# A five-stage image and text model on one core: which expert outputs are combined on TensorE, and how linear attention's contraction is split

## The reference

```python
# mixture of experts: G=8 groups of S=192 tokens, capacity C=60 a group and expert
gate, idx = top_k(softmax(x @ w_router), 2)
dispatch = one_hot(place_of_token_in_expert, C)
combine = dispatch * gate
expert_out = relu(einsum('gsec,gsd->egcd', dispatch, x) @ wi) @ wo
h = h + einsum('gsec,egcd->gsd', combine, expert_out)
# linear attention, 12 heads of 16
q, k, v = layernorm(h) @ w_qkv.T
q, k = q / max(sum_over_tokens|q|, eps), k / max(sum_over_tokens|k|, eps)
h = h + (q @ (k.T @ v)) @ w_proj.T + b_proj
```

## Time and profile before

| | us |
|---|---|
| median of three runs | 353.85 |
| lowest and highest of them | 352.6 and 359.36 |
| profiled execution, its own time | 351.75 |
| its span (first to last instruction) | 349.9 |

### The profile page before, as it was taken

The page is one execution under the profiler, slowest core; times in us unless marked ns, Lnnn a source line. Parts: engine busy times, 40 slices in busy tenths (PEclk is TensorE's granted clock), DMA queues, the critical chain, the costliest instruction groups (busy, mean ns, idle before and its releaser), DMA issues.

```text
span 349.9 us, 9294 instructions
## 1 busy us (share of the span) xinstructions
PE 319.5 (91%) x3966; PEld 216.6 (62%) x3966; DVE 193.6 (55%) x636; ACT 112.5 (32%) x218; POOL 52.4 (15%) x100
## 2 busy tenths in 40 slices
PE   3999899887788889999999999999998999998595
PEld 3876468655665336574747484756676576777465
DVE  2817487999999992141431110202045887789864
ACT  1233635665741352222222213030202232333250
POOL 8403233100111000000020000000028811101100
PEclk9999999999999999999999999999999999999899
DMA  7985011333120000505050505000002200000005
GB/s 254 350 238 146 5 37 36 116 108 125 54 55 3 2 0 2 153 7 156 3 157 2 157 2 157 4 21 24 0 25 65 53 20 0 3 2 0 2 0 135
DMA packets 16485, 23.45 MB, mean 67 GB/s; under 512 B 3995, under 2 KB 12573, under 8 KB 16445
## 3 DMA queue, kind: packets, MB, share of 16 engines
q1 hardware_dynamic: 14972, 21.10, 20.1%
q0 software_dynamic: 576, 1.18, 1.3%
q10 hardware_dynamic: 896, 0.59, 0.7%
HBM read 20.11 MB, written 2.75 MB: 65 GB/s over the span
## 4 chain that ended last, share of the span: by engine, by line
PE 64%; DVE 16%; SPq 8%; issue 4%; DMA 3%; POOL 2%; ACT 2%; DVEq 0%; POOLq 0%
PE banks L755 18%; PE banks L770 18%; PE banks L810 3%; PE banks L264 3%; SPq L288 2%; PE banks L818 2%; SPq L340 2%; PE banks L654 2%; PE banks L857 2%; PE banks L847 2%; PE banks L522 2%; DVE sb_onehot_combT L1729 2%; DVE sb_stat L1551 2%; POOL sb_onehot_combT L478 2%; SPq L286 1%
## 5 line engine op out<-in xcount | busy, mean ns | idle before, releaser
L755 PE MATMUL banks<-sb_tok_xeT,sb_wi_sl 128*128 128x480 f32 (+1 forms) x192 | 64.9, 590 | 1.1 <-ACT sb_tok_xeT L1264 1.1
L770 PE MATMUL banks<-sb_wo_sl,sb_attn_hidT_attn 128*60 128x192 f32 x768 | 64.1, 327 | 0.0
L770 PEld LDWEIGHTS banks<-sb_wo_sl,sb_attn_hidT_attn 128*60 128x60 f32 x768 | 52.9, 133 | 12.5 <-issue 4.0
L1279 ACT ACTIVATE sb_attn_hidT_attn<-banks 128x480 f32<-128x480 f32 x48 | 25.6, 569 | 95.7 <-PE banks L755 95.7
L755 PEld LDWEIGHTS banks<-sb_tok_xeT,sb_wi_sl 128*128 128x128 f32 (+1 forms) x192 | 24.8, 187 | 37.7 <-issue 35.8
L1777 DVE COPY sb_w_tok_e_out<-banks 60x384 f32<-60x384 f32 x16 | 8.9, 555 | 61.9 <-PE banks L770 61.6
L522 PE MATMUL banks<-sb_tok_xeT 128*32 128x193 f32 (+1 forms) x512 | 23.4, 328 | 0.0
L1779 DVE COPY sb_onehot_combT<-banks 60x384 f32<-60x384 f32 x16 | 8.9, 555 | 22.1 <-PE banks L770 22.0
L522 PEld LDWEIGHTS banks<-sb_tok_xeT 128*32 128x32 f32 (+1 forms) x512 | 15.8, 109 | 5.9 <-issue 2.3
L810 PE MATMUL banks<-sb_w_kv,sb_xnT 96*128 96x384 f32 x48 | 17.6, 497 | 1.0 <-ACT sb_xnT L1290 1.0
L1183 ACT ACTIVATE sb_onehot_combT<-sb_tok_xeT 128x1024 f32<-128x1024 f32 x8 | 8.5, 1059 | 21.7 <-DMA sb_tok_xeT<-in_xhalo 21.7
(11 more groups left out here) (262 smaller groups left out, 516.9 us busy)
## 6 DMA issues: line engine op xcount, KB each, us to landing
sb_wo_sl<-in_wo SPq DMA_DIRECT2D x8, 576.0 KB, 4.7
sb_tok_xeT<-in_xin SPq DMA_DIRECT2D x8, 448.0 KB, 5.4
sb_wi_sl<-in_wi SPq DMA_DIRECT2D x8, 288.0 KB, 3.1
sb_wi_sl<-in_wi SPq DMA_DIRECT2D x24, 96.0 KB, 3.1
sb_w_tok_e_out<-in_wtok SPq DMA_DIRECT2D x2, 960.0 KB, 7.2
expert_rows<-sb_onehot_combT SPq DMA_DIRECT2D x8, 192.0 KB, 4.4
sb_w_tok_e_out<-in_wtok SPq DMA_DIRECT2D x1, 576.0 KB, 8.4
out<-sb_h SPq DMA_DIRECT2D x8, 72.0 KB, 2.0
```

The source lines that it names most:

```text
L755: mm = nc.tensor.matmul(PS[:, banks[z], 0:SLOTS], lhs, rhs.rearrange("k g c -> k (g c)"), start=first, stop=not first)
L770: mm = nc.tensor.matmul(PS[64 * z:64 * z + CAP, 4 + hf, pr * D:(pr + 1) * D], hidT[:, e % 2, f, g * CAP:(g + 1) * CAP], wo_sl[:, q, f], st ...
L1279: nc.scalar.activation(hidT[:, e % 2, f], PS[:, HID_BANKS[(e * (FT // 2) + f // 2) % 2][f % 2], 0:SLOTS], ACT.Relu).then_inc(sem("hidT"), 1)
```

## The change

- `JC` is 1: only group 0 is combined on TensorE. Groups 1, 2 and 3 (`ROW_GROUPS = 3`) go through memory: rows of three groups are stored for each expert (288 KB in place of 192 KB), and 18 fetches are made, in the order of the groups. Three blocks of combine weights are built and turned in place of six, and `combine(1, ...)` with its two additions is gone. `keep_expert` makes four copies of 192 columns for the first half of an expert's results (group 0 to `e_out`, group 1 to `rows_out`) in place of two of 384. `rows_out` lies in another buffer and is cleared later.
- Linear attention's features are split as 128 + 64. `turn_linear` makes three transposes a block (the last 64 features are laid down twice, in partitions 0 to 63 and 64 to 127), the weights are loaded in the same way (15 transfers in place of 9), and `linear_keys_values` and `linear_queries` first do all products over 128 features and then those over 64, with neighbours in different halves of the array. Keys and values of a group are now one step of three blocks.
- `soft_norm` has two small operations ahead of the normalizing in place of five; the power is now of D times the variance, to +1/2 (the small constants change from TINY to TINY_VAR with it).
- PSUM banks, the waits ahead of TensorE's steps and the lists of TensorE, ScalarE, VectorE and GpSimd are new from the last expert on.

```diff
-JC = 2
+JC = 1
+ROW_GROUPS = J - JC
-LIN_T_BANKS, LIN_Q_BANKS, LIN_KV_BANKS = (0, 1), (1, 3), (1, 0, 4)
-PROD_BANK, SUM_BANK, LIN_O_BANKS, PROJ_BANKS = 4, 0, (1, 2), (3, 2)
+LIN_T_BANKS, LIN_Q_BANKS, LIN_KV_BANKS = (0, 1), (2, 3), (0, 4, 7)
+PROD_BANK, SUM_BANK, LIN_O_BANKS, PROJ_BANKS = 4, 1, (1, 2), (5, 3)
...
             def turn_linear(j):
+                src = xn_b[j % 2]
                 for blk in range(NB):
                     pe.wait_ge(sem("b_xn"), NB * j + blk + 1)
-                    for kh in range(2):
-                        mm = flip(PS[0:HD, LIN_T_BANKS[kh], blk * 128:(blk + 1) * 128], xn_b[j % 2][:, blk, kh * HD:(kh + 1) * HD])
+                    cols = slice(blk * 128, (blk + 1) * 128)
+                    flip(PS[:, LIN_T_BANKS[0], cols], src[:, blk, 0:128])
+                    flip(PS[:, LIN_T_BANKS[1], cols], src[:, blk, D - 128:D])
+                    mm = flip(PS[0:DT, LIN_T_BANKS[1], cols], src[:, blk, 128:D])
                 mm.then_inc(sem("b_xnT_ps"), 1)
-            def linear_keys_values(j, blk):
+            def linear_keys_values(j):
                 pe.wait_ge(sem("b_xnT"), j + 1)
-                for kh in range(2):
-                    mm = nc.tensor.matmul(PS[:, LIN_KV_BANKS[blk], 0:2 * D], xnT[:, kh, blk * 128:(blk + 1) * 128],
-                                          w_kv1[:, kh], start=(kh == 0), stop=(kh == 1))
-                mm.then_inc(sem("b_kv_ps"), 1)
+                for blk in range(NB):
+                    nc.tensor.matmul(PS[:, LIN_KV_BANKS[blk], 0:2 * D], xnT[:, 0, blk * 128:(blk + 1) * 128], w_kv1[:, 0],
+                                     start=True, stop=False)
+                for blk in range(NB):
+                    rows = slice(blk % 2 * DT, (blk % 2 + 1) * DT)
+                    nc.tensor.matmul(PS[:, LIN_KV_BANKS[blk], 0:2 * D], xnT[rows, 1, blk * 128:(blk + 1) * 128], w_kv1[rows, 1],
+                                     start=False, stop=True).then_inc(sem("b_kv_ps"), 1)
...
             for e in range(E):
                 expert_inner(e)
-                if 0 < e < 4:
-                    turn_comb(2 * e - 2)
-                    turn_comb(2 * e - 1)
+                if 0 < e < 3:
+                    for i in ((0, 1), (2,))[e - 1]:
+                        turn_comb(i)
                 expert_outer(e)
...
                         if hf == 0:
-                            ve.tensor_copy(e_out[64 * (e % 2):64 * (e % 2) + CAP, z:z + 3:2, e // 2], src).then_inc(sem("e_out"), 1)
+                            ve.tensor_copy(e_out[64 * (e % 2):64 * (e % 2) + CAP, z, e // 2], src[:, 0])
+                            ve.tensor_copy(mine[:, 0], src[:, 1]).then_inc(sem("e_out"), 1)
                         else:
-                            ins = ve.tensor_copy(rows_out[64 * z:64 * z + CAP, e % 2], src)
+                            ins = ve.tensor_copy(mine[:, 1:3], src)
...
-                then(ve.tensor_tensor(st[:, 6], mv[:, :, 1], st[:, 3], ALU.mult))
-                then(ve.scalar_tensor_tensor(st[:, 7], st[:, 6], float(D) ** 0.5, st[:, 2], ALU.mult, ALU.mult))
-                then(ve.tensor_scalar(st[:, 8], st[:, 7], L2_EPS, None, ALU.add))
-                then(ve.reciprocal(st[:, 9], st[:, 8]))
-                then(ve.tensor_tensor(st[:, 4], st[:, 9], st[:, 2], ALU.mult))
+                then(ve.scalar_tensor_tensor(st[:, 6], st[:, 2], L2_EPS, st[:, 3], ALU.mult, ALU.add))
+                then(ve.reciprocal(st[:, 4], st[:, 6]))
```

247 lines of the change are left out of this document (125 added, 122 removed).

## The result

| | before | changed |
|---|---|---|
| median of 7 runs each, us | 353.85 | 355.99 |
| lowest and highest, us | 352.05 to 359.36 | 354.36 to 357.76 |
| ratio of the two, 95% interval | | 1.0074 [1.0044, 1.0104] |
| profiled execution: own time, span, us | 351.75, 349.9 | 355.87, 354.0 |
| mean granted clock of that execution | 0.995 | 0.976 |

The change costs 0.7%, some 2.6 us, where 351.0 us was forecast; the time lies above the range of 346.5 to 355.5. In this table and the next the medians, lowest and highest times are of all runs, while the ratios leave out the slow ones, those over 1.5% above the fastest of the same kernel (one of the kernel before here, two of e4's four, nine of the 30 of the kernel before behind h1 to h4).

A forecast was written before the change was run, and what follows sets the result against it. GpSimd's queue of fetches and scales, not TensorE, was taken to decide what a removed combine is worth. Terms behind the experts summed to 0, experts saved 1.5: 351.75 - 1.5 = 350.2, plus 0.85 gave 351.0 us, range 346.5 to 355.5.

The forecast's parts named there:

- TensorE's clock: Wait ahead of first linear-attention turn: a clock fall worth 1.4 to 2 us, all but 0.3 hidden, left out of sum.
- Rival 3: Linear attention, groups 0 and 1: half clock set off by the 7.3 us wait stays; 356.5 us, chance 0.1.
- signs of being wrong: Idle under 4 us before first turn; half-clock stretch over 5 us; VectorE late at last norm by over 1 us.
- signs of being right: About 7 us idle before first turn; scale two fetches later; K/V(2) released by GpSimd's scale; K/V 3.4 to 3.5 us.
- The late fall may go: Near the last norms: idle time shrinks to about 2 us, which would give back 1.3 us; left out of sum.
- Store and first fetch, norm scale of group 0: Behind the experts: store +0.3 us, scale behind four fetches, TensorE waits 7.3 us, the step 3.0 us late.
- Contraction: Linear attention's 128+64 split: overlapping half products save net 0.56 us a group, 2.2 in all; K/V 3.45 for 3.95.
- Rival 2: Linear attention: halves don't overlap, a group costs 0.39 us more instead of 0.56 less; 353.4 us, chance 0.07.
- Groups 1 to 3: Linear attention: fetch queue and scales make group 1 1.9 us late; queries(3) done at 313.3 us against 311.3.
- Soft experts: Soft mixture after queries(3): shorter norm chain wins back 2.0 us; last norm ends at 328.8 where it was 328.88.
- rival 1: Whole kernel: TensorE is the bound throughout, its saved 8.3 us shows in full; 343.5 to 345 us, chance 0.15.
- Rival 4: Row fetches: 12 more blocks land later than 3.8 us behind their start, delaying groups 1 and 2; 352 us, chance 0.08.

The follow-up runs named there:

- e4: Changed kernel with groups 0 and 1 combined on TensorE and two groups' rows fetched, as before; 355.33 us, ratio 0.9918.
- h1: Kernel before, waits filled, with the first linear-attention turn moved ahead of group 1's combining, so TensorE waits; 356.18 us, ratio 1.0067.
- h4: Changed kernel as it is, measured again on another chip; 357.55 us, ratio 1.0088 to the kernel before.
- e1: Changed kernel with seven unread products filling the wait between combine(0) and the first linear-attention turn; 355.08 us, ratio 1.0012.
- f1: Changed kernel with unread products filling TensorE's waits at three places, seven of them behind combine(0); 350.88 us, ratio 0.9943.
- e3: Changed kernel with the contraction put back to 96 + 96 features in the new order of work; 359.06 us, ratio 1.0079.
- g2: Kernel before, waits filled, with the two-step norm and the 128 + 64 contraction in the old order of work; 354.19 us, ratio 1.0005.
- f4: Changed kernel with waits filled at three places, but soft_norm's five steps as before; 352.0 us, ratio 0.9952.
- f3: Changed kernel with two groups combined on TensorE as before and the two other waits filled; 351.54 us, ratio 0.9941.
- h3: Kernel before with its waits filled, measured again in a later batch; 350.8 us, ratio 0.9899.
- e2: Changed kernel with the norm scale of group 0 behind two fetches, as before, and not four; 354.4 us, ratio 0.9965.
- g3: Changed kernel with waits filled at three places, but three products in place of seven ahead of the first linear-attention turn; 353.81 us, ratio 0.9968.

## Why the prediction was wrong

**The step that failed is "TensorE's clock".** It saw the fall coming, priced it at 1.4 to 2 us of work, let the waits behind it hide "all but some 0.3", and left it out of the sum. Measured (changed against e1 and f1): 3.42 us at K/V(1), 2.87 us at turn_soft(3). Both halves of the estimate were off. The size came from the one stretch in the trace of before, 3.4 us long; this one was 10.2, and it cost 0.98 us from the first turn to the first key product (3.22 for 2.24) and 2.42 on K/V(0) (6.01 for 3.59), with queries(0) back at full clock. And what was to hide it did not: only 0.56 us were absorbed, between K/V(1) and K/V(2). turn(1) and K/V(1) were taken as held by GpSimd and VectorE until 277.9 and 280.4. By the walk's own terms TensorE was through with group 0 at 277.45 (270.65 + 3.45 + 2.15 + 1.2), so the first of these holds left 0.45 us of slack for a delay of 1.4 to 2. In the trace turn(1) starts at 280.67 right behind TensorE's slow work, and the chain stays on TensorE from there. The hold on VectorE's side moved too: it has the key norms of group 0 ahead of group 1's norm and stood 2.77 us for the slow products (row 277.92 above). Work that is said to hide a delay must not depend on what is delayed. The Trainium skill's rule ("TensorE: Matmul & The Clock Gate", section "HAM oscillation — how this bites in real kernels"), that a burst behind too long a wait starts at half clock, was cited and then given no weight in the sum. The trace agrees with it: the burst behind the wait of 7.00 us began at half clock.

**Rival 3 came closest**: slower, 356.5 us against 355.99, chance 0.1. Its direction held (the half clock stays on behind the wait), but the nearness of the number is luck. It has the half clock last through 15 us of TensorE's work, at 0.5 us each, less 2 of slack; the measured one lasted through less than 5 (the first turn and K/V(0)), cost 3.4, and found 0.56 of slack. By the rival's own scale 4 us of work would have shown nothing. Its price of one half was too low: the twelve passes of the earlier trace rows take 2.84 us for 1.48, which is 0.9 us more for each us of work. Nor did its reason hold: the clock stayed low to the end of the 10.2 us though TensorE ran without a gap from 271.17 on. Its argument against itself, that before the clock came back within 3.4 us, was read from a single stretch; e1, e3 and e4 show the same late place with 10.2 us.

**The signs of being wrong** that the prediction names came true in two of three: a half-clock stretch of over 5 us (10.2), and VectorE late at the last norm by over 1 us (2.08). Of its signs of being right, the wait (7.00) and the scale's place held, and K/V(2) is released by GpSimd's scale only with the clock whole (f1), not in the changed kernel itself.

**"The late fall may go"**: it didn't, in any unfilled version profiled; a wait of 2.08 us in place of 3.19 was no cure.

**Expert stage, -1.5**: measured -1.46 (130.88 to 129.42), in every pair of profiles.

**Store and first fetch, norm scale of group 0**: first fetch +0.3 and the scale behind four fetches, wait of 7.3: measured +0.22 (4.32 us behind the first combining for 4.10) and 7.00, with 11.07 us from the first combining to the turn (forecast 11.3).

**Contraction**: 0.56 us a group, K/V 3.45: measured 0.34 of work and 0.43 at turn_soft(3) by e3, K/V 3.60. Rival 2 (no overlap of the halves) is false for this order, and true for the old one, by g2.

**Groups 1 to 3**: with the clock whole (f1) K/V(1) stands 22.82 us behind the first combining, by the walk 280.5 - 257.18 = 23.3; K/V(2) 34.62, by the walk 34.6; then the walk runs ahead: K/V(3) 48.73 against 48.1, outputs(3) 63.16 against 61.8.

**Soft experts, "the 2.0 us are won back"**: turn_soft(3) was to stay at 71.1 and is at 72.49 in f1, so 1.4 us too hopeful. All of it had been lost before outputs(3) (63.16 against 61.8), in the work of groups 2 and 3 that the walk listed too short: 14.1 us from K/V(2) to K/V(3) for 13.5, and 14.4 from there to outputs(3) for 13.7. The norm's shorter chain is worth 1.17 us by f4.

**Rivals 1 and 4**: rival 1 asked for 343.5 to 345 us; even with the clock whole it is 350.9 (f1), whose chain runs through the queue of fetches. Rival 4 (later landings) is false: from issue to landing a fetch takes 2.7 us in the median both before and after (part 6 of the pages). The 3.8 us that the walk took for every landing was the one in the chain.

In sum, by the profiles against the kernel before: experts -1.46, linear stage and norms +1.3 (forecast 0), clock behind the opened wait +2.9 (forecast 0), tail +0.2: +2.9 against -1.5 forecast. What stays open: why executions have 3.4 or 10.2 us (late), or 10.2 or 13.7 (opened wait), at half clock in the same place; where the gains of the computing parts go in f3; and whether the change makes the stretch near 109 us likelier. That one is in the changed kernel's profile (the first 8 in the clock row above) and not in that of before, but the code there is the same, and one profile of before decides nothing.

**A version better than both**: f2, the kernel before with its waits filled (0.9894, and 0.9899 in h3), and g4, the changed one with a filled wait and an earlier scale (0.9899 [0.9832, 0.9966]). These can't be told apart.

## What to carry to other kernels

An operation that looks like cost may be what keeps TensorE at full clock: before taking work out, look whether it leads into a wait, and price the wait with the clock behind it. If the wait can't be closed, products that nobody reads, written to a free bank, can keep the clock whole at no cost, as long as they end before the wait does and fill most of it (three of seven, with 4.22 us of wait left, did not help). A part that gains within a new order of work may gain nothing over the old order: set it against the old kernel too. When a kernel's runs scatter by a per cent, look at the granted clock of each stretch first, and compare distances inside the profiles, or versions with the waits filled, rather than times.

## What was not expected of the hardware

- The length of a wait doesn't tell the length of the stretch at half clock behind it. It was 3.4 us behind 3.19 (before), 2.08 (changed, late) and 4.36 us (h1); 10.2 us behind 7.00 (changed), 5.63 (e2), 4.22 (g3) and 2.07 us (e1, late); and 13.7 us in h4 behind 7.00 us again. One of 6.8 us came near 111 us in e1. Behind 1.14 us (g4) and less at these places the clock stayed whole. The fall need not come within the wait: at the late place of the kernel before the wait ended at 328.35, the transposes behind it ran at full clock, and the fall came at 329.7.
- Half products of 64 rows cost 0.84 us when each follows a whole product, and 0.50 when three follow one another (1.49).
- Filled with products in its waits, the kernel before is 1.0% faster and its eight runs lie within 3.1 us (h3), where 30 of the unfilled in that batch spread over 8.9 us. Filling these places is no guarantee: f3's ten runs spread over 8.9 us too.
